# A first narrow cross-attention on one core: transposing the probabilities, or computing the scores twice

## The chip, the cores and the metric

The kernel is one program on one core of a Trainium2 chip. The metric is the device time of one execution, in microseconds (us); lower is better. TensorE (PE) multiplies matrices out of SBUF into PSUM, which has eight banks of 128 x 512 numbers; VectorE (DVE) and ScalarE (ACT) read PSUM; GpSimd (POOL) works on SBUF alone. The engines run side by side, each through its own instructions in order, and wait for each other by semaphores.

## The reference, cut to what matters

Four cross-attention layers follow each other on 32 batches of 128 tokens and 128 features, with a context of 128 x 96 per batch. The change is in the attention of the second layer, which has 16 heads of 8 features:

```python
q = (x @ Wq + bq)   # heads of 8: q[h], k[h], v[h]
k = (xf @ Wk + bk)
v = (xf @ Wv + bv)
scores = einsum('bhqd,bhkd->bhqk', q * SCALE, k)
probs = softmax(scores, axis=-1)
attn = einsum('bhqk,bhkd->bhqd', probs, v)
out = attn @ Wo + bo
```

Then come a layer norm, a feed-forward and the residual, which the change leaves alone. All numbers are float32.

## The kernel before

The program has four stages: the two wide attentions of the first layer (`wide_attention`), its feed-forward, the narrow attention of the second layer (`narrow_attention`, called with `L1` tiles) with its feed-forward, and the last two layers together (`wide_and_narrow`). The change replaces `narrow_attention`, which nothing else calls.

`narrow_attention` is a software pipeline over the batches. In step t each engine does its part of several batches, and each engine's list of parts is written out by hand in a function `step`; a loop (`pipeline`, `Fori`) runs two steps per turn between a written-out beginning and end. The steps' parts are these:

- POOL copies x of batch t+3 (`copy_rows`, L1231) and its context (`stage_context`, L1236), and makes `k_apart` of batch t+2 (`set_keys_apart`, L1242): four copies of the keys, in copy j all rows zero but those of head j of each group of four heads.
- PE transposes x (`transpose_h`, L1077), projects queries, keys (L1048, L1049) and values (L1054), and makes the scores of batch t+1 (`score`, L1028): four matmuls of 32 rows by 512 columns, one in each 32-row group of the array, into four banks.
- DVE takes the row maxima of 16 heads in two halves (`row_maxima`, L1167), negates the first half (L1174) and subtracts the second half from the scores (`subtract_maxima`, L1178).
- ACT takes the exponentials, the first eight heads one at a time with the maximum as bias (L1120), the other eight in one instruction (L1127). The result has queries on the partitions.
- PE transposes the 16 probability tiles (`transpose_probs`, L1040), and ACT copies them out, four tiles per copy (`turned_probs`, L1113).
- PE multiplies by a tile of ones for the sums and by the values (`weigh`, L1069: 16 matmuls each, four column groups of the array at a time). DVE inverts the sums (L1191) and multiplies (L1194). PE applies Wo (L1081), and DVE adds the bias into `y` (L1203).

Four PSUM banks hold the scores; the other four are a ring (`Ring`), filled in the order of the list `order`. PE may fill a ring bank once the engine that reads its earlier content has emptied it.

Of the kernel before, what the change touches and what calls it, by code (L numbers as in the profile page):

```python
# [19 lines left out]
HEADS = 16  # L20
# [113 lines left out]
def build(nc, a, out):  # L134
    ctx = ExitStack()
    with ctx:
# [797 lines left out]
def narrow_attention(nc, N, x, dst, ctxT, ident, head_mask, waits):  # L934
# [3 lines left out]
    order = [("T0", 0, "act"), ("T1", 0, "act"), ("Wo", -1, "dve"), ("T2", 0, "act"), ("T3", 0, "act"),  # L938
             ("qk", 2, "act"), ("v", 1, "dve"), ("hT", 3, "dve"), ("sum", 0, "dve"), ("PV", 0, "dve")]
    first, last = -3, BATCHES  # L940
    steady_first, steady_last = 3, BATCHES - 4
    ring = Ring(order, range(first, last + 1), BATCHES, {})
    GROUP = 4
    QUAD = DIM // 4
    SKEW = QUAD + NARROW

    def here(at, lag):
        return 0 <= at.n + lag < BATCHES

    with ExitStack() as ctx:  # L950
# [6 lines left out]
        rows_h = sb("rows_h", [TOKENS, DIM])  # L957
        hT = sb("hT", [DIM, 2, TOKENS])
        cT = sb("cT", [N.kv_rows, 2, TOKENS])
        qT = sb("qT", [128, 2, TOKENS])  # L960
        kT = sb("kT", [128, 2, TOKENS])
        k_apart = sb("k_apart", [128, 2, GROUP, TOKENS])
        v = sb("v", [TOKENS, 2, 4, 4 * SKEW])
        ones = sb("ones", [TOKENS, 4 * SKEW])
        invT = sb("invT", [128, TOKENS])
        oT = sb("oT", [128, TOKENS])
        probs = sb("probs", [TOKENS, 2, 2, SLOT_HEADS, TOKENS])
        probsT = sb("probsT", [TOKENS, HEADS, TOKENS])
        table_loader = sb("table_loader", [TOKENS, 1])
        row_max = sb("row_max", [TOKENS, 2, SLOT_HEADS])  # L970
        neg_max = sb("neg_max", [TOKENS, SLOT_HEADS])
        scores = ctx.enter_context(nc.psum_tensor(f"{N.name}_scores", [TOKENS, 2, 2, GROUP, TOKENS], FP32))
        ring_banks = ctx.enter_context(nc.psum_tensor(f"{N.name}_ring", [128, Ring.BANKS, BANK], FP32))

        filled = {"act": sem("ring_filled_act"), "dve": sem("ring_filled_dve")}
        emptied = {"act": sem("ring_emptied_act"), "dve": sem("ring_emptied_dve")}
        rows_h_ready = sem("rows_h_ready")
        cT_ready = sem("cT_ready")
        scores_full = sem("scores_full")
        max_ready = [sem("max_ready_0"), sem("max_ready_1")]  # L980
        neg_max_ready = sem("neg_max_ready")
        shifted = sem("shifted")
        exp_ready = [sem("exp_ready_0"), sem("exp_ready_1")]
        keys_apart = sem("keys_apart")
        cleared = sem("cleared")
        ones_ready = sem("ones_ready")
        block = ctx.enter_context(nc.Block())

        def bank(name, at):
            return ring_banks[:, ring.bank(name, at), :]  # L990

        def await_filled(engine, name, at):
            engine.wait_ge(filled[ring.engine[name]], ring.count(name, at))

        def await_emptied(engine, name, at):
            engine.wait_ge(emptied[ring.engine[name]], ring.count(name, at))

        def steps(engine, step):
            pipeline(engine, step, first, last, steady_first, steady_last)

        def by_group(tile):
            return tile.rearrange("p (j k) -> p j k", k=SKEW)

        @block.tensor
        def _(pe):
            keep_clock(nc, scores[:, 0, 0, 0, :], ident, START_COUNT)
# [3 lines left out]
            def start_fill(name, at):  # L1010
                before = ring.before(name, at)
                if before:
                    pe.wait_ge(emptied[before[0]], before[1])
                return bank(name, at)

            def filled_by(instruction, name):
                instruction.then_inc(filled[ring.engine[name]], 1)

            def score(at):
                pe.wait_ge(keys_apart, at.times(1, 1))  # L1020
                if at.n >= 1:
                    pe.wait_ge(exp_ready[0], at.times(2, 0))
                    pe.wait_ge(shifted, at.times(1, 0))
                p = at.n % 2
                for g in range(4):
                    r, s = divmod(g, 2)
                    part = slice(QUAD * g, QUAD * (g + 1))
                    last = nc.tensor.matmul(scores[:, s, r, :, :], qT[part, p, :], k_apart[part, p, :, :],  # L1028
                                            start=True, stop=True, tile_position=(QUAD * g, 0))
# [1428 lines left out]
```

## Time and profile before

| what | us |
|---|---|
| median of 3 runs (lowest, highest) | 1704.61 (1701.34, 1705.19) |
| profiled execution, span from first to last instruction | 1703.5 |
| the narrow attention of the second layer in it: first instruction 845.4, last row of y | 1060.0 |

No other time is given for the profiled execution, so its span stands for it: it is 1.1 us under the median and within the runs. The page of the profile gives busy times over the whole span; what belongs to the changed stage is read from views of the stretch from 845 to 1061 us. In rows of groups, "x32" counts instructions, then come busy us and mean ns, and behind the second bar the idle time in front of them. PE's records are matmuls; every float32 matmul has two records, since it runs as two passes, each with a weight load (PEld) of its own; a transpose has one.

### The profile page before, as it was taken

How to read it: one execution, taken by the hardware profiler on the slowest of the kernel's cores; microseconds unless marked ns; L12 is line 12 of the kernel's file. 1: busy time of each engine (PE TensorE's matmuls, PEld its weight loads, DVE VectorE, ACT ScalarE, POOL GpSimd, SP SyncE). 2: the span in 40 equal slices, each digit the busy share in tenths (PEclk: the TensorE clock that was granted, in tenths of full speed). 3: DMA queues.
4: the chain of work that ended last, by engine and by line, in shares of the span. 5: the costliest groups of instructions: out<-in, count | busy, mean ns of one | idle time of the engine just before them, and what ended most of it. 6: DMA issues, size and time to landing. Idle time of an engine off the chain costs nothing. (4 is left out here: it accounts for less than half of the span.)

```text
span 1703.5 us, 49104 instructions
## 1 busy us (share of the span) xinstructions
PE 1641.7 (96%) x16560; PEld 1355.9 (80%) x16560; DVE 1306.9 (77%) x2406; ACT 1244.3 (73%) x3865; POOL 677.1 (40%) x946
## 2 busy tenths in 40 slices
PE   7999999999999999989999998997999999999997
PEld 6888888888888888879877776876888888888876
DVE  5877777767777777747588887656888888888884
ACT  4777777767777777733388887446888888888886
POOL 3444444444444444423222221644444344443440
PEclk9999999999999999999989999999999999999999
DMA  6777777777776777630000000004443444344440
GB/s 183 199 195 188 188 188 186 210 201 210 197 186 186 186 183 196 186 95 1 0 2 0 0 0 1 1 13 140 125 141 116 142 126 139 118 140 122 133 130 8
DMA packets 225223, 211.27 MB, mean 124 GB/s; under 512 B 19474, under 2 KB 222804, under 8 KB 225108
## 3 DMA queue, kind: packets, MB, share of 16 engines
q1 hardware_dynamic: 225108, 209.92, 44.5%
q8 instruction: 49, 0.80, 0.2%
q14 instruction: 66, 0.54, 0.1%
HBM read 109.72 MB, written 100.14 MB: 123 GB/s over the span
## 5 line engine op out<-in xcount | busy, mean ns | idle before, releaser
L691 ACT ACTIVATE L_probs<-L_scores,L_neg_max 128x128 f32<-128x128 f32 x512 | 182.7, 386 | 135.7 <-DVE L_neg_max L783 135.7
L907 POOL TENSOR_TENSOR L_probs<-L_probs,L_inv_sum 128x1024 f32<-128x1024 f32 x128 | 242.8, 1897 | 88.7 <-DVE L_inv_sum L803 88.7
L777 DVE TENSOR_REDUCE L_row_max<-L_scores 128x8 f32<-128x1024 f32 x128 | 156.2, 1220 | 44.2 <-PE L_scores L549 44.2
L2122 POOL TENSOR_TENSOR L2L_w_probs<-L2L_w_probs,L2L_w_inv_sum 128x1024 f32<-128x1024 f32 x64 | 121.4, 1896 | 125.7 <-DVE L2L_w_inv_sum L1925 125.4
L809 DVE STREAM_TRANSPOSE L_squares<-L_probs 128x1024 f32<-128x1024 f32 x125 | 153.0, 1224 | 0.3 <-POOL L_probs L907 0.3
L549 PE MATMUL L_scores<-L_kT,L_qT 64*128 64x128 f32 x2048 | 132.5, 279 | 0.9 <-ACT L_kT L680 0.9
L600 PE MATMUL L_ring<-L_probsT,L_v 128*64 128x128 f32 x2048 | 127.5, 277 | 5.3 <-issue 2.5
L600 PEld LDWEIGHTS L_ring<-L_probsT,L_v 128*64 128x64 f32 x2048 | 111.2, 137 | 25.3 <-issue 20.3
L549 PEld LDWEIGHTS L_scores<-L_kT,L_qT 64*128 64x128 f32 x2048 | 120.1, 189 | 12.6 <-ACT L_oT L680 8.1
L793 DVE TENSOR_REDUCE L_sums<-L_probs 128x8 f32<-128x1024 f32 x64 | 78.1, 1220 | 66.3 <-ACT L_probs L698 66.3
L1689 ACT ACTIVATE L2L_w_probs<-L2L_scores,L2L_w_neg_max 128x128 f32<-128x128 f32 x256 | 90.4, 371 | 40.3 <-DVE L2L_w_neg_max L1889 40.3
L691 ACT ACTIVATION_READ_ACCUMULATOR L_probs<-L_scores,L_neg_max 128x1 f32 x512 | 115.8, 226 | 0.0
L680 ACT ACTIVATE L_oT<-L_ring 128x512 f32<-128x512 f32 x128 | 76.5, 599 | 42.0 <-PE L_ring L600 42.0
L1878 DVE TENSOR_REDUCE L2L_w_row_max<-L2L_scores 128x8 f32<-128x1024 f32 x64 | 76.6, 1197 | 24.4 <-PE L2L_scores L1444 24.4
L1700 ACT ACTIVATE L2L_n_probs<-L2L_scores,L2L_n_neg_max 128x128 f32<-128x128 f32 x256 | 90.7, 377 | 5.5 <-DVE L2L_n_neg_max L1895 4.9
L1242 POOL TENSOR_TENSOR L_k_apart<-L_kT,quad_mask 128x512 f32<-128x512 f32 x32 | 33.3, 1040 | 151.6 <-ACT L_kT L1113 151.6
L1113 ACT ACTIVATE L_probsT<-L_ring 128x512 f32<-128x512 f32 x128 | 75.3, 616 | 24.2 <-PE L_ring L1040 22.2
L1167 DVE TENSOR_REDUCE L_row_max<-L_scores 128x8 f32<-128x1024 f32 x64 | 78.1, 1220 | 18.9 <-PE L_scores L1028 18.9
L680 ACT ACTIVATE L_kT<-L_ring 128x512 f32<-128x512 f32 x128 | 76.8, 600 | 18.5 <-PE L_ring L557 18.5
L680 ACT ACTIVATE L_qT<-L_ring 128x512 f32<-128x512 f32 x128 | 76.2, 595 | 16.7 <-PE L_ring L557 11.4
L1040 PEld LDWEIGHTS L_ring<-ident,L_probs 128*128 128x128 f32 x512 | 57.0, 143 | 37.2 <-issue 21.3
L2098 POOL TENSOR_TENSOR L2L_n_x_bias<-L2L_n_rows_h,bias_L 128x128 f32<-128x128 f32 x32 | 14.6, 456 | 177.0 <-DVE x L1974 176.8
(227 smaller groups left out, 4644.1 us busy)
## 6 DMA issues: line engine op xcount, KB each, us to landing
L_relay<-L_squares SPq DMA_DIRECT2D x125, 512.0 KB, 3.4
L_probsT<-L_relay SPq DMA_DIRECT2D x500, 128.0 KB, 3.7
L2L_relay<-L2L_w_squares SPq DMA_DIRECT2D x62, 512.0 KB, 3.6
L2L_w_probsT<-L2L_relay SPq DMA_DIRECT2D x248, 128.0 KB, 2.9
out_x<-x SPq DMA_DIRECT2D x32, 64.0 KB, 2.7
L0a_wq<-in_L_xattn_Wq SPq DMA_DIRECT2D x2, 256.0 KB, 2.9
L0a_wk<-in_L_xattn_Wk SPq DMA_DIRECT2D x2, 256.0 KB, 3.7
L0a_wv<-in_L_xattn_Wv SPq DMA_DIRECT2D x1, 512.0 KB, 6.3
```

Source lines behind the costliest of these rows:

```text
L549: last = nc.tensor.matmul(scores[:, s, r, i, :], q[part, i, at.n % 2, :], k[part, i, at.n % 2, :], start=True, stop=True, tile_position=(h ...
L600: last = nc.tensor.matmul(to[WIDE * r:WIDE * (r + 1), TOKENS * i:TOKENS * (i + 1)], v[:, at.n % 2, WIDE * h:WIDE * (h + 1)], probsT[:, at. ...
L680: nc.scalar.activation(to, src, ACT.Copy).then_inc(emptied["act"], 1)
L691: done = nc.scalar.activation(slot_probs(at, 0)[:, n, :], scores[:, 0, r, i, :], ACT.Exp, scale=layer_of(at).scale, bias=neg_max[:, n:n + ...
L777: nc.vector.tensor_reduce(row_max[:, s, :], slot(s), AX.X, ALU.max).then_inc(max_ready[s], 1)
L793: nc.vector.tensor_reduce(sums[:, :, 1, :], slot_probs(at, 1).rearrange("p (r i) k -> p r i k", r=2), AX.X, ALU.add).then_inc(sum_ready, 1)
L809: nc.vector.transpose(squares[:, at.n % 2, :, SLOT_HEADS * s:SLOT_HEADS * (s + 1), :] .rearrange("p j h a -> p h j a"), slot_probs(at, s). ...
L907: nc.gpsimd.tensor_tensor(to, to, inv_sum[:, :, s, :].unsqueeze(3) .to_broadcast([TOKENS, 2, GROUP, TOKENS]), ALU.mult).then_inc(divided, 1)
L1167: nc.vector.tensor_reduce(row_max[:, s, :], scores[:, s, :, :, :].rearrange("p r i k -> p (r i) k"), AX.X, ALU.max).then_inc(max_ready[s], 1)
L1689: done = nc.scalar.activation(w_slot(at, 0)[:, h, :], scores[:, 0, r, i, :], ACT.Exp, scale=W.scale, bias=w_neg_max[:, h:h + 1], accum_out ...
L1700: done = nc.scalar.activation(n_slot(at, 0)[:, h, :], scores[:, 0, r, i, :], ACT.Exp, scale=N.scale, bias=n_neg_max[:, h:h + 1], accum_out ...
L2122: nc.gpsimd.tensor_tensor(to, to, w_inv_sum[:, :, s, :].unsqueeze(3) .to_broadcast([TOKENS, 2, GROUP, TOKENS]), ALU.mult).then_inc(w_divid ...
```

## The change

`narrow_attention` goes, and the second layer calls `text_attention`. It has the same inputs and outputs and does the softmax in another way:

- Scores are made a first time with queries on the partitions, only for the maxima (`scores_for_max`); DVE takes the maxima of four heads at a time, negated (`find_maxima`, 128 x 512).
- The 16 maxima per query are transposed (`turn_maxima`) and added into rows of the queries that were zero (`append_maxima`); the matching rows of `k_apart` are ones. A second matmul (`scores_less_max`) then gives the scores less their maximum directly, with keys on the partitions: what ACT's exponential makes of them (`exponentiate`, four heads each) goes into the product with the values without a transpose.
- The values have a column of ones, so one product (`weigh`) gives sums too. Its result is transposed back (`turn_back_and_out`), divided on rows (`divide_and_finish`), transposed again (`turn`) and multiplied by Wo.
- Three PSUM banks take scores for the maxima, three scores less maxima, one (`a_bank`) in turn the product, the transposes and the projections for ACT, and one (`b_bank`) the maxima and the transposes back for DVE.
- PE's step begins with two mixed passes (`both_scores`) right behind each other: the first makes groups 0 and 1 of the first scores of batch t+2 and groups 2 and 3 of the second scores of batch t, the second the other groups.
- The 40 steps are written out; there is no loop.

The core of the diff:

```diff
-            narrow_attention(nc, text, x, y, ctxT, ident, quad_mask, [(loaded["L1"], loads["L1"])])
+            text_attention(nc, text, x, y, ctxT, ident, quad_mask, [(loaded["L1"], loads["L1"])])
...
-def narrow_attention(nc, N, x, dst, ctxT, ident, head_mask, waits):
...
+def text_attention(nc, N, x, dst, ctxT, ident, quad_mask, waits):
...
+    S_BANKS = T_BANKS = 3
+    T_ORDER = (2, 3, 0, 1)
+    STEPS = range(-5, BATCHES + 3)
...
+            def scores_for_max(b, g, h):
+                part = slice(QUAD * g, QUAD * (g + 1))
+                if h == 0:
+                    if g == 0:
+                        pe.wait_ge(parts_ready, b + 1)
+                    if 4 * b + g >= S_BANKS:
+                        pe.wait_ge(max_ready, 4 * b + g + 1 - S_BANKS)
+                last = nc.tensor.matmul(s_bank(b, g)[:, 2 * (1 - h):2 * (1 - h) + 2, :],
+                                        q_part[part, b % 4, h, :], k_apart[part, b % 4, 2 * h:2 * h + 2, :],
+                                        start=True, stop=True, tile_position=(QUAD * g, 0))
+                if h == 1:
+                    last.then_inc(s_full, 1)
+
+            def scores_less_max(b, g, j):
+                part = slice(QUAD * g, QUAD * (g + 1))
+                if j == 0:
+                    pe.wait_ge(b_empty, nth_b["mT", b - 1])
+                    if t_nth(b, g) >= T_BANKS:
+                        pe.wait_ge(exp_ready, t_nth(b, g) + 1 - T_BANKS)
+                last = nc.tensor.matmul(t_bank(b, g)[:, j, :], k_apart[part, b % 4, j, :],
+                                        q_part[part, b % 4, j // 2, :],
+                                        start=True, stop=True, tile_position=(QUAD * g, 0))
...
+            def both_scores(t, s_groups, t_groups):
+                for h in range(2):
+                    if real(t + 2):
+                        for g in s_groups:
+                            scores_for_max(t + 2, g, h)
+                    if real(t):
+                        for j in (2 * h, 2 * h + 1):
+                            for g in t_groups:
+                                scores_less_max(t, g, j)
...
+            def weigh(t):
+                b = t - 1
+                pe.wait_ge(exp_ready, 4 * b + 4)
+                pe.wait_ge(a_empty, nth_a["PV", t] - 1)
+                for half in range(2):
+                    for e in range(2):
+                        for c in range(4):
...
+            def turn(t):
+                if nth_a["turn", t] > 1:
+                    pe.wait_ge(a_empty, nth_a["turn", t] - 1)
+                if real(t + 5):
+                    last = nc.tensor.transpose(a_bank[:, 0, :], x[:, t + 5, :], ident[:, :])
+                if real(t - 2):
+                    pe.wait_ge(b_empty, nth_b["D", t - 1])
+                    last = nc.tensor.transpose(a_bank[:, 1, :], rows_o[:, :, :].rearrange("p h d -> p (h d)"),
+                                               ident[:, :])
+                last.then_inc(a_full, 1)
...
+            def project(t):
+                pe.wait_ge(a_empty, nth_a["qkv", t] - 1)
...
+            for t in STEPS:
+                both_scores(t, (0, 1), (2, 3))
+                both_scores(t, (2, 3), (0, 1))
+                if ("mT", t) in nth_b:
+                    turn_maxima(t)
+                if ("PV", t) in nth_a:
+                    weigh(t)
+                if ("turn", t) in nth_a:
+                    turn(t)
+                if ("D", t) in nth_b:
+                    turn_back_and_out(t)
+                if ("qkv", t) in nth_a:
+                    project(t)
...
+            def exponentiate(b, g):
+                act.wait_ge(t_full, t_nth(b, g) + 1)
+                nc.scalar.activation(exps[:, b % 2, GROUP * g:GROUP * (g + 1), :].rearrange("p h q -> p (h q)"),
+                                     t_bank(b, g).rearrange("p j q -> p (j q)"), ACT.Exp,
+                                     scale=N.scale).then_inc(exp_ready, 1)
...
+            for t in STEPS:
+                if real(t):
+                    exponentiate(t, 2)
+                    exponentiate(t, 3)
+                    exponentiate(t, 0)
+                if ("PV", t) in nth_a:
+                    weighed_out(t)
+                if real(t):
+                    exponentiate(t, 1)
+                if ("turn", t) in nth_a:
+                    turned(t)
+                if ("qkv", t) in nth_a:
+                    projected(t)
...
+            for t in STEPS:
+                if real(t + 2):
+                    find_maxima(t + 2, 0)
+                    find_maxima(t + 2, 1)
+                if ("mT", t) in nth_b:
+                    append_maxima(t)
+                if real(t + 2):
+                    find_maxima(t + 2, 2)
+                if ("D", t) in nth_b:
+                    divide_and_finish(t)
+                if real(t + 2):
+                    find_maxima(t + 2, 3)
...
+            def set_parts(b):
+                pool.wait_ge(a_empty, nth_a["qkv", b - 4])
+                if b >= 4:
+                    pool.wait_ge(t_full, 4 * (b - 4) + 4)
+                for j in range(GROUP):
+                    other = (j + 2) % GROUP
+                    nc.gpsimd.tensor_scalar(k_apart[:, b % 4, j, :], qk[:, b % 2, 1, :], quad_mask[:, j:j + 1],
+                                            quad_mask[:, other:other + 1], ALU.mult, ALU.add)
+                for n in range(2):
+                    done = nc.gpsimd.tensor_scalar(q_part[:, b % 4, n, :], qk[:, b % 2, 0, :], half_mask[:, n:n + 1],
+                                                   half_bias[:, n:n + 1], ALU.mult, ALU.add)
+                done.then_inc(parts_ready, 1)
```

`weighed_out`, `turned` and `projected` are ACT's copies out of `a_bank`: 128 x 256, 128 x 256, and 128 x 128 with 128 x 256. Each of the product, `turn` and `project` waits until ACT has copied the one before it out (`a_empty`).

## Rows read from the trace of the kernel before

**Rows 1.** Tile y; busy time in a stretch: us, busy us and count by engine, granted clock

```profile
L1203 DVE TENSOR_TENSOR y<-L_ring,bias_L x32: 283/292/293, 866.9 to 1060.0; 128x128 f32 x26, 128x128 f32<-128x128 f32 x6
...
852.00:1061.00 209.00, 201.12 (x3097) 154.53 (x3094) 178.85 (x288) 179.22 (x479) 46.04 (x90) 0.98 0.00 1
```

**Rows 2.** Timeline of the beginning of the stage (start us, us, then the group)

```profile
847.27 0.14 PEld L1077 LDWEIGHTS L_ring<-ident,L_rows_h 128*128 128x128 f32 x1
847.38 0.27 PE L1077 MATMUL L_ring<-ident,L_rows_h 128*128 128x128 f32 x1
...
850.49 2.09 PE L1028 MATMUL L_scores<-L_k_apart,L_qT 32*128 32x512 f32 x8 [1.63 <-POOL L_k_apart L1242]
```

**Rows 3.** Timeline of one step

```profile
952.95 1.14 PE L1028 MATMUL L_scores<-L_k_apart,L_qT 32*128 32x512 f32 x8
...
954.74 1.04 PE L1040 MATMUL L_ring<-ident,L_probs 128*128 128x128 f32 x8
...
957.55 1.06 PE L1069 MATMUL L_ring<-L_probsT,L_v 128*32 128x128 f32 x32
```

**Rows 4.** Groups of instructions by line and shape, 852 to 1061 us

```profile
L1167 DVE TENSOR_REDUCE L_row_max<-L_scores 128x8 f32<-128x1024 f32 x64 | 78.1, 1220 | 18.9 <-PE L_scores L1028 18.9
L1113 ACT ACTIVATE L_probsT<-L_ring 128x512 f32<-128x512 f32 x128 | 75.3, 616 | 24.2 <-PE L_ring L1040 22.2
L1178 DVE TENSOR_TENSOR L_probs<-L_scores,L_row_max 128x1024 f32<-128x1024 f32 x32 | 39.2, 1225 | 1.1
L1191 DVE RECIPROCAL L_invT<-L_ring 128x128 f32<-128x128 f32 x32 | 30.4, 949 | 2.4 <-PE L_ring L1069 2.4
L1113 ACT ACTIVATE L_kT<-L_ring 128x128 f32<-128x128 f32 x31 | 8.8, 284 | 0.0
```

**Rows 5.** Waits from 852 to 1061 us: total us, times, longest

```profile
DVE L_row_max L1167 <- PE L_scores L1028: 18.9, 32, 3.5
```

**Rows 6.** One line's instructions: ns min/median/max, first and last start

```profile
L836 DVE COPY L_probsT<-L_ring x3: 692/692/692, 729.8 to 744.3; 128x512 f32<-128x512 f32 x3
```

**Rows 7.** Groups of the whole program, by line and shape

```profile
L2372 DVE SCALAR_TENSOR_TENSOR L0ff_hidden<-L0ff_value,bp,L0ff_gelu 128x256 f32<-128x256 f32 x64 | 29.6, 478 | 12.5 <-ACT L0ff_gelu L2322 9.5 <-PE L0ff_value L2283 2.3
L803 DVE RECIPROCAL L_inv_sum<-L_sums 128x8 f32<-128x8 f32 x128 | 23.4, 183 | 2.8 <-ACT L_probs L691 0.4
L698 ACT ACTIVATE L_probs<-L_probs 128x1024 f32<-128x1024 f32 x64 | 67.4, 1052 | 0.0
L1231 POOL COPY L_rows_h<-x 128x128 f32 x26 | 7.6, 294 | 0.0
L2414 POOL TENSOR_TENSOR L0ff_rstd<-L0ff_var_eps,minus_half 128x2 f32<-128x2 f32 x16 | 11.3, 704 | 1.3
```

**Rows 8.** The page's DMA queues: packets, MB, share of 16 engines

```profile
q8 instruction: 49, 0.80, 0.2%
```

**Rows 9.** Timeline at the end of the stage

```profile
1059.14 0.29 DVE L1194 TENSOR_TENSOR L_oT<-L_ring,L_invT 128x128 f32<-128x128 f32 x1
1059.48 0.30 PEld L1081 LDWEIGHTS L_ring<-L_wo,L_oT 128*128 128x128 f32 x2 [0.80 <-DVE L_oT L1194]
...
1060.01 0.29 DVE L1203 TENSOR_TENSOR y<-L_ring,bias_L 128x128 f32<-128x128 f32 x1 [0.58 <-PE L_ring L1081]
```

**Rows 10.** Timeline of the wide attention: column-tiled matmuls, then row-tiled ones

```profile
720.52 1.97 PE L600 MATMUL L_ring<-L_probsT,L_v 128*64 128x128 f32 x32
...
722.41 1.86 PEld L549 LDWEIGHTS L_scores<-L_kT,L_qT 64*128 64x128 f32 x32 [0.17 <-issue]
722.41 2.06 PE L549 MATMUL L_scores<-L_kT,L_qT 64*128 64x128 f32 x32
```

**Rows 11.** Busy time by stretch, columns as in the first group

```profile
850.40:854.40 4.00, 3.88 (x15) 1.97 (x15) 1.72 (x3) 0.63 (x3) 0.29 (x3) 0.50 0.01 4
1680.00:1690.00 10.00, 7.15 (x80) 5.44 (x79) 9.21 (x13) 8.65 (x35) 1.04 (x1) 1.00 0.01 1
```

More of the change, by code:

```diff
@@ L931, in _, with real, numbered @@
             steps(pool, step, before_loop)
-def narrow_attention(nc, N, x, dst, ctxT, ident, head_mask, waits):
[L938 to L942, printed above, removed]
+def text_attention(nc, N, x, dst, ctxT, ident, quad_mask, waits):
     GROUP = 4
     QUAD = DIM // 4
-    SKEW = QUAD + NARROW
-    def here(at, lag):
-        return 0 <= at.n + lag < BATCHES
+    SKEW = 48
+    SPAN = 2 * NARROW
+    PAIRS = HEADS // 2
+    S_BANKS = T_BANKS = 3
+    T_ORDER = (2, 3, 0, 1)
+    STEPS = range(-5, BATCHES + 3)
+    def real(b):
+        return 0 <= b < BATCHES
+    def numbered(parts):
+        return {name_t: n + 1 for n, name_t in enumerate(
+            (name, t) for t in STEPS for name, lags in parts if any(real(t + lag) for lag in lags))}
+    nth_a = numbered((("PV", (-1,)), ("turn", (5, -2)), ("qkv", (4, 1))))
+    nth_b = numbered((("mT", (1,)), ("D", (-1, -3))))
     with ExitStack() as ctx:
@@ L955, in sem @@
             return ctx.enter_context(nc.semaphore(f"{N.name}_{name}"))
[L957 to L966, printed above, removed]
@@ L1016, in filled_by @@
[L1016 to L1029, printed above, removed]
-                last.then_inc(scores_full, 1)
@@ L1106, in _ @@
-            steps(pe, step)
+            def scores_for_max(b, g, h):
[10 more added lines that the diff above has]
+                    last.then_inc(s_full, 1)
@@ new lines, in weigh @@
+            def weigh(t):
[5 more added lines that the diff above has]
+                        for c in range(4):
+                            pair = 4 * half + c
+                            last = nc.tensor.matmul(a_bank[QUAD * c:QUAD * (c + 1), half, :],
+                                                    v[:, b % 2, pair, :, :].rearrange("p e k -> p (e k)")
+                                                    [:, QUAD * e:QUAD * (e + 1)],
+                                                    exps[:, b % 2, 2 * pair + e, :],
+                                                    start=e == 0, stop=e == 1, tile_position=(0, QUAD * c))
+                last.then_inc(a_full, 1)
@@ new lines, in turn_back_and_out @@
+            def turn_back_and_out(t):
+                pe.wait_ge(b_empty, nth_b["D", t] - 1)
+                if real(t - 3):
+                    pe.wait_ge(a_empty, nth_a["turn", t - 1])
+                    last = nc.tensor.matmul(b_bank[:, 2, :], hoT[:, (t - 1) % 2, 1, :], N.wo[:, :],
+                                            start=True, stop=True)
+                if real(t - 1):
+                    pe.wait_ge(a_empty, nth_a["PV", t])
+                    for half in range(2):
+                        last = nc.tensor.transpose(b_bank[:, half, :], weighed[:, half, :], ident[:, :])
+                last.then_inc(b_full, 1)
@@ L1110, in _ @@
             nc.scalar.activation(table_loader[:, :], ident[:, 0:1], ACT.Exp)
-            def copied(to, src):
-                nc.scalar.activation(to, src, ACT.Copy).then_inc(emptied["act"], 1)
-            def exponentiate_0(at, r):
-                if r == 0:
-                    act.wait_ge(neg_max_ready, at.times(1, 1))
-                for i in range(GROUP):
-                    n = GROUP * r + i
-                    done = nc.scalar.activation(probs[:, at.n % 2, 0, n, :], scores[:, 0, r, i, :], ACT.Exp,
-                                                scale=N.scale, bias=neg_max[:, n:n + 1])
-                done.then_inc(exp_ready[0], 1)
@@ L1153, in _, with weighed_out @@
-            steps(act, step)
+            def exponentiate(b, g):
[3 more added lines that the diff above has]
+                                     scale=N.scale).then_inc(exp_ready, 1)
+            def weighed_out(t):
+                act.wait_ge(a_full, nth_a["PV", t])
+                nc.scalar.activation(weighed[:, :, :].rearrange("p b q -> p (b q)"),
+                                     a_bank[:, 0:2, :].rearrange("p b q -> p (b q)"), ACT.Copy).then_inc(a_empty, 1)
@@ L1260, in wide_and_narrow @@
+            for b in range(BATCHES):
+                set_parts(b)
 def wide_and_narrow(nc, W, N, x, ctxT, ident, minus_half, eps, head_mask, waits, store):
```

307 lines of the change are left out of this document (103 added, 204 removed).

## The prediction

> **What bounds the kernel now.** I found the stage by its output: y's 32 rows start from 866.9 to 1060.0 us [rows 1], so a step takes (1060.0 − 866.9)/31 = 6.23 us. Then the busy times of the stretch, in the same group: PE 201 of 209 us, DVE and ACT 179 each, POOL 46, no DMA. PE's figure is too high, since its records contain the way out of the array. One transpose takes 0.27 [rows 2], eight in a row 1.04 [rows 3]: a pass of 128 columns holds the array for (1.04 − 0.27)/7 = 0.11 us and needs 0.16 more to come out. In the same group the scores (eight passes of 512 columns, 1.14) are two rounds of 0.43, so four passes run together, one in each row group; the product with the values (32 passes, 1.06) is eight rounds of 0.11. PE's need per step is thus 16 × 0.11 for transposed probabilities, 0.86 for scores, 2 × 0.88 for sums and values and nine passes of 0.11 for the rest: 5.4 us. DVE has 179/209 × 6.23 = 5.3 us, of it two maxima at 1.22, the subtraction at 1.23 and the reciprocal at 0.95 [rows 4]. What DVE waits for is mainly the scores, 18.9 us in 32 waits, 0.6 per step [rows 5]. DVE is the bound, nearly closed by that wait.
>
> **The change, engine by engine.** *DVE*: four maxima of 512 columns cost 0.69 each, as a 512-column copy out of PSUM does [rows 6] (half of 1.22, 0.61, is the low end). The two additions of maxima, 128 columns each: such an instruction takes 0.48 for 256 columns [rows 7], less 128 × (1.22 − 0.69)/512 = 0.13 gives 0.35. In the same group a reciprocal of 8 takes 0.18; with 0.95 for 128, one of 16 takes 0.23. y 0.29 [rows 1], the multiplication on rows the same. Sum 4.25, down from 5.3. *ACT*: four exponentials of 512 at 0.61 (a copy of 512 takes 0.616 [rows 4], and an exponential of 1024 takes 1.05 [rows 7], so the function costs nothing extra); three copies of 256 columns at 0.40, a third of the way from 0.284 for 128 to 0.616 for 512 [rows 4]; a copy of 128. Sum 3.9. *PE*: 16 transposes and the ones go; scores are made twice, 1.72 if four groups always run together; maxima 0.11, product 0.88, two transposes 0.22, two back and Wo 0.44, projections 0.66. Sum 4.0, down from 5.4. *POOL*: six instructions of 128 columns, between a copy's 0.29 and the dearest small operation's 0.70 [rows 7]: 1.7 to 4.2 us, I take 0.4 each. They have more than a step from a projection to the scores that need it, so they cost nothing; over 6.8 us they would be the bound, and no row comes near. No DMA moves, and SP's queue is not passed. The 40 steps written out add code; the instruction queue was busy for 0.2% [rows 8], so I take nothing, and as upper bound one more gap of issue per step, 0.17 as in [rows 10].
>
> **What sets the step afterwards** is no engine but a chain PE–ACT–PE, because `a_bank` is used three times per step and PE waits for ACT between uses, and because the second mixed pass waits for what the first starts. Prices of the links: DVE ends at 1059.43, PE's load starts 1059.48, and DVE has the result of two passes at 1060.01 [rows 9]: 0.58 = 0.05 handoff + 0.11 load + 0.22 + 0.16 out + 0.04. The load in front of a matmul that had to wait is seen bare in 847.27 to 847.38 [rows 2]. A change of the array's division costs too: column-tiled records end at 722.49, so the last stream at 722.33, and the row-tiled load starts at 722.41 [rows 10]: 0.09 + 0.11 = 0.20. From the end of the second mixed pass (0):
>
> - change 0.20, maxima transposed 0.11; change 0.20, product 0.88: 1.39
> - out 0.20, ACT's copy 0.40: 1.99 (ACT's third exponential is done by 0.8; the fourth runs behind this copy and hides)
> - handoff and load 0.16, two transposes 0.22, out 0.20, copy 0.40: 2.97 (the transposes back and Wo, 0.44, lie beside this copy)
> - 0.16, six projection passes 0.66: 3.79; change 0.20: 3.99. ACT's last copies end at 4.6, before they matter
> - first mixed pass 0.86: 4.85
> - out 0.20, maxima of group 0 on DVE 0.69, handoff and load 0.16: 5.90. Here PE stands before group 3 of the first scores: it has three banks, and the fourth group needs the bank of group 0 of the same batch. Behind this wait on PE's queue stand the second scores of groups 0 and 1 (which wait for the first exponential, 0.20 + 0.61 + 0.16 = 0.97 against 1.05), hence ACT's last two exponentials and the whole list above. DVE reaches those maxima in time: its divide ends at about 3.7, the last maxima at 4.4
> - rest of the second pass 0.86: 6.76.
>
> So the step is **6.8 us** against 6.23, although every engine has less to do: PE idles 2.8 us of it. Thirty of 40 steps are full. Before them PE must turn x, project, let POOL set parts and make two batches of scores, one thing behind the other, mostly at half clock as the old beginning does (scores at 2.09 instead of 1.14 [rows 2, 3], granted clock 0.50 [rows 11]): turn until 848.0, turn and projection until 849.9, POOL until 852.4, scores of batch 0 with the wait until 857.1, turn and projection until 859.8, batch 1 until 863.4, two turns: first full step at 865. After the full steps: step 30 lacks scores for maxima and four projection passes (6.3), step 31 (2.7 of scores), then two products' chains (7.4) until y: 16.3. y's last row would start at 865 + 30 × 6.8 + 16.3 = 1085.3, and did at 1060.0: **+25 us**. The profiled span, 1703.5, is 1.1 under the median; on the median this gives 1704.6 + 25 = 1730.
>
> Unknown is the mixed pass itself: the trace has no matmuls of 256 and 128 columns side by side in different row groups. Not below 0.86, since each group has four rounds' worth of columns; at most about 1.9, if two passes of one matmul must both start before the next matmul (0.22 + 0.22 per matmul of 256, 0.11 + 0.11 of 128, partly overlapped). I take 0.86, as four equal passes do run together [rows 3], and keep the rest for the range. A second doubt is whether weights of 128 columns load in time for passes of only 128. In the wide attention 32 passes in two row groups take 2.06, so 16 in each group follow at 0.11, with a load of 128 columns for each [rows 10]: the load is hidden behind the same group's pass. The Trainium skill (TensorE: Matmul & The Clock Gate, Part 3) says that a weight load overlaps matmuls in flight only where the row group differs. By that rule each of the second scores' passes would cost 0.22, a mixed pass 1.7 and the step 8.4; the row speaks against it.
>
> **Rivals.** *Mixed passes run less than four abreast*, because starts keep program order and a short matmul stands behind a long one's second pass. Mild (pairs regroup, 1.08): step 7.0, 865 + 210 + 16 = 1091, 1736 us. Full (1.9, the first scores of group 0 done at 1.3): step 7.85, 1761 us. For it: nothing in the trace shows unequal ones overlapping; against: rounds of four equal ones start together. The same page of the Trainium skill, in the same part, has matmuls strictly first in, first out. Chance 0.24.
>
> *Weight loads not hidden* in the mixed pass: step 8.4, 865 + 252 + 16 = 1133, 1778 us. This is the rule named above; by [rows 10] I give it 0.04.
>
> *The clock falls.* With PE streaming 4.0 of 6.8 us the granted clock could drop to 1.2 GHz as in the beginning; streams and loads double, the step is about 11.2, 1860 us. Against: 1680 to 1690 us has PE records for 7.2 of 10 us, and clock 1.00 [rows 11]. Chance 0.05.
>
> *Faster, by hidden changeovers.* If PE loaded weights across the three changes of division (3 × 0.20) and ahead of the waits (3 × 0.11), the step would be 6.76 − 0.93 = 5.8, the start 862: 862 + 175 + 16 = 1053, 1698 us. It decides below a step of 5.97, where 865 + 30 × 5.97 + 16 is 1060. For it: in a row of transposes no load shows; against: [rows 9, 10] show each exposed. Chance 0.06. With most of these savings, a step near 6.0, there is no change: 0.05.
>
> That the change doesn't do what it says I leave out: the transposes and the subtraction are gone from the code.
>
> **How the numbers follow.** Forecast 0.56; its own range is a step of 6.5 to 7.1, 1721 to 1739. The first rival reaches to 1761; with a little over half of the changeovers hidden the step is 6.2 and the time 1712. Range 1712 to 1762, which leaves out the load rule, the clock, faster and no change, 0.20. Smaller than 0.2% (3.4 us), about what a measurement of this kernel tells from nothing, counts as no change. Faster 0.06, same 0.05, slower 0.89.
>
> **What the changed profile would show.** Right: y's rows 6.8 apart; in each step a PE wait of about 1 us on DVE's maximum between the mixed passes, and two on ACT's copies of `a_bank`; DVE and ACT busy for under 70% of the stage; clock 1.00. Wrong: rows of y under 6 apart, mixed passes far longer than 0.9, POOL named as releaser, or clock 0.50 in full steps.

## The result, and the profile after

| | before | after |
|---|---|---|
| median, us (executions) | 1702.97 (4) | 1736.80 (4) |
| lowest to highest | 1700.52 to 1705.19 | 1729.53 to 1744.12 |
| ratio of the times, 95% interval | | 1.0208 [1.0167, 1.0250] |
| span of the profiled execution | 1703.5 | 1742.4 |
| last row of y of the stage in it | 1060.0 | 1097.0 |

The change costs 34 us, 2.1%; the forecast was 1730. The profiled execution of after took 1744.12, the longest of its four. Its span grew by 38.9; y's last row stands 37.0 later, and what follows it took 1.9 more. But the stage also began earlier there. It starts from the last rows of x, which DVE wrote at 844.33 before and at 839.15 after:

```profile
844.33 0.42 DVE L2379 TENSOR_TENSOR x<-L0ff_out,L0ff_base 128x256 f32<-128x256 f32 x1 [2.21 <-PE L0ff_out L2292]
...
839.15 0.42 DVE L2361 TENSOR_TENSOR x<-L0ff_out,L0ff_base 128x256 f32<-128x256 f32 x1 [2.21 <-PE L0ff_out L2274]
```

From there to y's last row the stage takes 215.7 us before and 257.9 after: it grew by 42.2 in this execution, and the part ahead of it was 5.2 shorter. That part is the same code; in the traces of the old attention below it ends at 838.3 to 844.3, so such a difference comes from the execution. Times of the stage are therefore counted from these rows of x where two traces are compared.

Tile y, first over the whole stage, then from 905 to 1000 us alone, and in the same stretch before:

```profile
L1193 DVE TENSOR_TENSOR y<-L_b_bank,bias_L x32: 227/227/290, 897.8 to 1097.0; 128x128 f32<-128x128 f32 x32
...
L1193 DVE TENSOR_TENSOR y<-L_b_bank,bias_L x13: 227/227/229, 911.4 to 993.4; 128x128 f32<-128x128 f32 x13
...
L1203 DVE TENSOR_TENSOR y<-L_ring,bias_L x15: 292/292/292, 904.8 to 994.0; 128x128 f32 x15
```

In the middle the rows stand (993.4 − 911.4)/12 = 6.83 us apart, and stood (994.0 − 904.8)/14 = 6.37 apart before (the forecast's 6.23 is an average with the lighter first and last steps). The second thing to see is at both ends: the first row came 30.9 later than in [rows 1]. A part of that is the deeper pipeline, which writes the row of batch b in step b + 3 and not in step b + 1; another part is the granted clock. Columns of the next view: stretch, us, busy us (instructions) of PE, PEld, DVE, ACT and POOL, granted clock, DMA share, GB/s.

```profile
852.00:862.00 10.00, 8.48 (x35) 5.27 (x33) 4.11 (x8) 0.98 (x4) 2.59 (x6) 0.50 0.00 0
862.00:872.00 10.00, 9.29 (x81) 7.79 (x82) 3.21 (x7) 3.40 (x9) 4.06 (x10) 0.50 0.00 0
872.00:884.00 12.00, 11.50 (x105) 8.67 (x106) 4.82 (x10) 4.47 (x10) 3.72 (x9) 0.50 0.01 3
884.00:897.00 13.00, 11.79 (x143) 9.18 (x138) 4.85 (x11) 4.80 (x11) 2.59 (x6) 0.65 0.01 1
...
905.00:1000.00 95.00, 83.19 (x1300) 65.44 (x1298) 51.13 (x124) 48.85 (x112) 36.29 (x84) 1.00 0.01 2
...
1064.00:1097.30 33.30, 27.50 (x333) 21.37 (x333) 9.55 (x30) 12.28 (x29) 1.39 (x4) 0.70 0.01 1
```

From 852 to past 884 TensorE ran at 1.2 GHz (0.50), through three full steps, and again in part of the end; the middle ran at 2.4 GHz (1.00), with DVE busy for 54% and ACT for 51% of it, against 86% each in [rows 1]. PE's records, which contain the way out of the array, fill 88% of it. No engine is full, and the waits between engines show in the step. One step of it in the timeline (start us, us, then the group; in brackets the idle time before and its releaser):

```profile
953.05 0.48 PE L1014 MATMUL L_s_banks<-L_k_apart,L_q_part 32*128 32x256 f32 x2
...
953.37 0.38 PE L1014 MATMUL L_s_banks<-L_k_apart,L_q_part 32*128 32x256 f32 x2
...
953.58 0.38 PE L1014 MATMUL L_s_banks<-L_k_apart,L_q_part 32*128 32x256 f32 x2
...
954.21 1.29 DVE L1175 TENSOR_REDUCE L_maxima<-L_s_banks 128x4 f32<-128x512 f32 x2 [0.83 <-PE L_s_banks L1014]
954.33 1.09 ACT L1119 ACTIVATE L_exps<-L_t_banks 128x512 f32<-128x512 f32 x2 [0.62 <-PE L_t_banks L1026]
954.96 0.18 PEld L1014 LDWEIGHTS L_s_banks<-L_k_apart,L_q_part 32*128 32x128 f32 x1 [0.71 <-DVE L_maxima L1175]
...
956.24 0.33 PE L1047 MATMUL L_b_bank<-ident,L_maxima 128*128 128x128 f32 x1
...
956.50 1.08 PE L1058 MATMUL L_a_bank<-L_exps,L_v 128*32 128x128 f32 x32
...
957.65 0.38 ACT L1125 ACTIVATE L_weighed<-L_a_bank 128x256 f32<-128x256 f32 x1 [0.83 <-PE L_a_bank L1058]
...
958.08 0.14 PEld L1069 LDWEIGHTS L_a_bank<-ident,x 128*128 128x128 f32 x1 [0.77 <-ACT L_weighed L1125]
...
958.56 0.38 ACT L1131 ACTIVATE L_hoT<-L_a_bank 128x256 f32<-128x256 f32 x1
...
958.99 0.30 PEld L1091 LDWEIGHTS L_a_bank<-L_hoT,L_wq 128*128 128x128 f32 x2 [0.27 <-ACT L_hoT L1131]
...
959.86 0.48 PE L1014 MATMUL L_s_banks<-L_k_apart,L_q_part 32*128 32x256 f32 x2
```

From 953.05 to 959.86 is 6.81. PE's three waits are where the forecast put them: 0.71 for the first maximum between the mixed passes (the forecast said about 1), 0.77 for ACT's copy of the product, 0.27 for its copy of the turned rows. In the waits of the whole stage (total us, times, longest) DVE waits for scores as in [rows 5], for longer, and now PE waits for DVE's maximum and for ACT's copies as well:

```profile
DVE L_maxima L1175 <- PE L_s_banks L1014: 35.0, 32, 3.3
...
PEld L_s_banks L1014 <- DVE L_maxima L1175: 22.5, 31, 1.5
PEld L_a_bank L1069 <- ACT L_weighed L1125: 20.4, 26, 1.0
...
PEld L_a_bank L1091 <- ACT L_hoT L1131: 10.0, 30, 1.1
```

### The profile page after: what moved, and what is told of

Same layout as the page of the kernel before. It is cut to its first block and busy times, and to the rows that moved or that the text cites. A ratio compares the mean times of both kernels' runs of the same rounds, so it can differ in the third digit from the quotient of the medians.

```text
span 1742.4 us, 47955 instructions
## 1 busy us (share of the span) xinstructions
PE 1662.4 (95%) x16432; PEld 1372.4 (79%) x16432; DVE 1247.9 (72%) x2406; ACT 1177.9 (68%) x3648; POOL 712.2 (41%) x1045
## 5 line engine op out<-in xcount | busy, mean ns | idle before, releaser
L777 DVE TENSOR_REDUCE L_row_max<-L_scores 128x8 f32<-128x1024 f32 x128 | 156.1, 1219 | 41.6 <-PE L_scores L549 41.6
L1175 DVE TENSOR_REDUCE L_maxima<-L_s_banks 128x4 f32<-128x512 f32 x128 | 84.7, 684 | 42.7 <-PE L_s_banks L1014 42.6
L1231 POOL TENSOR_SCALAR L_k_apart<-L_qk,quad_mask 128x128 f32<-128x128 f32 x128 | 55.5, 448 | 142.0 <-ACT L_qk L1146 142.0
L1119 ACT ACTIVATE L_exps<-L_t_banks 128x512 f32<-128x512 f32 x128 | 72.7, 595 | 54.4 <-PE L_t_banks L1026 54.4
L1014 PE MATMUL L_s_banks<-L_k_apart,L_q_part 32*128 32x256 f32 x512 | 97.8, 448 | 10.6 <-ACT L_exps L1119 8.2
```

The lines of the kernel that those rows point to most:

```text
L777: nc.vector.tensor_reduce(row_max[:, s, :], slot(s), AX.X, ALU.max).then_inc(max_ready[s], 1)
L1014: last = nc.tensor.matmul(s_bank(b, g)[:, 2 * (1 - h):2 * (1 - h) + 2, :], q_part[part, b % 4, h, :], k_apart[part, b % 4, 2 * h:2 * h + 2 ...
```

## The experiments

All times below were taken beside executions of the kernel before (medians 1700.6 to 1703.1); behind a time stand its ratio to them and the 95% interval. "The changed kernel" is after; diffs are against it unless they say otherwise.

### The changed kernel again, and with the clock held

> The changed kernel again, nothing edited, as the base for the others. My theory: the step stays 6.82 us, and what differs between executions (1730 and 1743 us so far) is only how long PE runs at half clock in the first and last steps of this stage; so a profile near 1730 shows a first stretch of granted clock 0.50 that ends some 10 us or more before the 893.3 of the profile seen, with y's rows still 6.82 apart in the middle. Rival: the step itself differs between executions (6.4 against 6.8 would be 13 us over 30 steps); then rows of y in the middle stand closer in a faster execution. Time: 1728 to 1746, median near 1737.

Five executions took 1729.66 to 1743.23, median 1739.06, ratio 1.0213 [1.0190, 1.0236]. The profiled one is the fastest of them. Its tile y, and its busy times by stretch, columns as above:

```profile
L1193 DVE TENSOR_TENSOR y<-L_b_bank,bias_L x32: 227/228/291, 893.0 to 1086.9; 128x128 f32<-128x128 f32 x32
```

```profile
872.00:884.00 12.00, 11.02 (x147) 8.58 (x147) 5.34 (x12) 5.00 (x11) 4.75 (x11) 0.77 0.02 4
884.00:897.00 13.00, 11.09 (x176) 8.67 (x164) 6.94 (x16) 6.54 (x16) 5.19 (x12) 1.00 0.00 1
```

Its clock is back at 1.00 about 15 us earlier (0.77 and 1.00 where the slower execution had 0.50 and 0.65), and y ends 10.1 earlier (the stage takes 246.8 us for 257.9). Its rows in the middle stand 6.82 apart but for two gaps of 6.97 and 6.96, so the step is not what differs.

> The changed kernel with 2 to 4 unused passes of 128 columns in front of each of PE's waits in the beginning (five steps) and in the last five steps of the stage; nothing else moves. My theory, half clock in the beginning and the end is what the forecast mis-sized: the granted clock stays 1.00 from 845 on, the first three full steps take 6.8 instead of 7.9, 10.3 and 10.6 (8.4 us less), the beginning itself 2 to 4 less, the end 2 to 5 less; first row of y 885 to 889 instead of 898; time 10 to 16 below the profiled 1744, so 1727 (1722 to 1733), and executions agree within 4 us. Rival one, the first full steps are slow for another reason (instructions not yet fetched, POOL's parts late): the clock is 1.00 but these steps still take 8 to 10; time within 4 us of the changed kernel's. Rival two, extra passes don't hold the clock: 0.50 as before, and the time is 1 to 4 us longer.

```diff
+            def warm(t, count):
+                if t < 0:
+                    keep_clock(nc, t_banks[:, 2, 0, :], ident, count)
+                if t >= BATCHES - 2:
+                    keep_clock(nc, s_banks[:, 0, 0, :], ident, count)
...
+                warm(t, 2)
                 if ("turn", t) in nth_a:
                     turn(t)
...
+                warm(t, 2)
                 if ("qkv", t) in nth_a:
                     project(t)
```

(Four more stand ahead of the first scores and of the second pass in the beginning, two ahead of the transposes back in the end.) Measured: 1728.01 (1726.62 to 1730.01), 1.0147 [1.0124, 1.0169]. Tile y, and the busy times of the beginning:

```profile
L1207 DVE TENSOR_TENSOR y<-L_b_bank,bias_L x32: 227/228/292, 884.7 to 1081.7; 128x128 f32<-128x128 f32 x32
```

```profile
842.00:852.00 10.00, 9.46 (x75) 7.98 (x74) 2.15 (x4) 1.70 (x6) 5.21 (x12) 1.00 0.00 0
852.00:862.00 10.00, 9.40 (x97) 7.30 (x96) 5.17 (x11) 3.13 (x9) 5.23 (x12) 1.00 0.01 2
```

The clock stayed at 1.00 but for 3.4 us each at 863 and 1064; the first rows of y came at 884.7, 13.1 earlier than in after's profile, and 6.8 apart from the first on. The median is 11.1 below the repeated changed kernel's, and the spread fell from 13.6 to 3.4 us. So holding the clock is worth about 11 us of the change's 36 here, and the clock is what makes executions differ.

25 us are left with the clock held, and the longer step is under half of them. In the profiles the stage takes 243.0 us against 215.7 before, 27.3 more. Of these 8.4 lie between x's last rows and step 0 (19.5, before 11.1 to the first transpose of batch 0's probabilities at 855.39), 10.9 in steps 0 to 29 (858.20 to 1061.28, before 855.39 to 1047.60), and 8.0 behind them. So the beginning and the end of the new pipeline, which is two steps deeper, cost more than its steps do; how much of the 8.0 is the unused passes' I did not measure on this version.

### The passes apart

> The second mixed pass is moved behind the product with the values, and ACT's third and fourth exponential behind its copy of the turned rows; the work is the same. My theory, the chain PE-DVE-PE between the passes and PE-ACT-PE through a_bank: mT and the product (1.39 with changes of division) lie in the 1.05 of waiting for the first maximum, and the second pass lies in the wait for ACT's copy of the product. Step: first pass 0.86, to the product's end 2.25, second pass 3.31, turn 3.73, out and copy and handoff 0.76 to 4.49, projections 0.66 and a change 0.20 to 5.35. So rows of y 5.35 to 5.6 apart, no wait of PE for a maximum in the middle of a step, the time 30 x (6.82 - 5.4) = 43 below the changed kernel's, about 1694 (1686 to 1701). Rival one, the work of PE or the loads of weights set the step: 6.6 or more, 1730. Rival two, the wait only moves (DVE's maxima or ACT's exponentials become late at another place): 6.2 to 6.5, 1719 to 1728.

```diff
                 both_scores(t, (0, 1), (2, 3))
-                both_scores(t, (2, 3), (0, 1))
                 if ("mT", t) in nth_b:
                     turn_maxima(t)
                 if ("PV", t) in nth_a:
                     weigh(t)
+                both_scores(t, (2, 3), (0, 1))
```

(On ACT the order becomes exponentials 2 and 3, `weighed_out`, `turned`, exponentials 0 and 1.) Measured: **1681.46** (1679.38 to 1681.70), 0.9869 [0.9848, 0.9891]: 58 below the repeated changed kernel, and 1.3% below before. Tile y from 905 to 1000 us, and the timeline of one step:

```profile
L1193 DVE TENSOR_TENSOR y<-L_b_bank,bias_L x18: 227/227/229, 909.7 to 999.0; 128x128 f32<-128x128 f32 x18
```

```profile
953.48 0.33 PE L1047 MATMUL L_b_bank<-ident,L_maxima 128*128 128x128 f32 x1
...
953.74 1.08 PE L1058 MATMUL L_a_bank<-L_exps,L_v 128*32 128x128 f32 x32
...
954.75 0.48 PE L1014 MATMUL L_s_banks<-L_k_apart,L_q_part 32*128 32x256 f32 x2
...
955.85 0.33 PE L1069 MATMUL L_a_bank<-ident,x 128*128 128x128 f32 x1
...
956.76 0.30 PEld L1091 LDWEIGHTS L_a_bank<-L_hoT,L_wq 128*128 128x128 f32 x2 [0.27 <-ACT L_hoT L1131]
```

Rows of y stand (999.0 − 909.7)/17 = 5.25 apart, 1.57 less for the same instructions: two of the three waits are gone, and the 0.27 for the turned rows is the one that is left. My count said 5.35. Both rivals fall, and the time lies under the range I gave. Between the kept traces the stage takes 193.1 us instead of the 246.8 of the faster changed execution, 53.7 less: 30 x 1.57 = 47 by the step, 3 more in the first of these steps, whose clock was back at 867 us, 11 earlier, and 4 in the beginning and the end.

> Both edits of the two kernels before this one: the mixed passes apart and unused passes in the beginning and the end. My theory has them independent: 43 from the step and 8 to 14 from the clock, about 1685 (1677 to 1692), 1% below the kernel before the change. Rival: the clock is gained by the denser steps anyway (the unused passes add nothing to the apart version): within 3 us of the apart version alone.

Measured: 1677.27 (1675.85 to 1682.94), 0.9854 [0.9831, 0.9876]. The median is 4 below the apart version, which itself had come 13 below its expectation, but the two intervals overlap, and in the kept traces the stage takes 192.2 us for 193.1. So the unused passes add far less than the 8 to 14 I gave them, and the rival is not excluded. The traces show why: y's first row came 3.9 earlier, counted from x's last rows (877.8 against 883.4, of which 1.6 lie ahead of the stage), but the unused passes at the end stretched the last seven rows by 3, where the apart version's clock had been 1.00 anyway.

> The version with the mixed passes apart and unused passes in the beginning only: in the version with both, those at the end made the last seven rows of y take 3 us longer (the apart version's clock was at 1.00 there already), while those in the beginning brought the first row from 883.5 to 877.8. My theory, both effects add: 1681.5 - 5.7 = 1676, or 1677.3 - 2.9 = 1674, so 1675 (1671 to 1680), and the last row of y at 1028 to 1029. Rival, without passes at the end the clock falls there: last row at 1031 or later, 1678 or more.

Measured, with the passes in the steps before step 0 alone: **1673.51** (1668.44 to 1677.72), 0.9829 [0.9806, 0.9852], 1.7% below the kernel before and the lowest median here, though its interval overlaps those of the two versions above. Rows of y run from 877.0 to 1027.1, and the stage takes 189.1 us: the 3 at the end came back, and the rival falls.

### What each wait of the chain is worth

The next three were executed once each (1743.23, 1736.47 and 1721.89), and their times contain how long the clock stayed down; they are read by the rows of y from 905 to 1000 us, where it was 1.00.

> The changed kernel with ACT's copy of the product out of a_bank made twice (the first into a spare tile), 0.38 us more of ACT in each step, ACT being busy for half of the time. My theory, PE stands before the turn until that copy ends: rows of y 7.20 apart instead of 6.82 (7.15 to 7.25), the stage 30 x 0.38 = 11 longer, PE's wait for the weighed tile 0.77 + 0.38 = 1.15. Rival, the wait is covered by something else that ends nearly as late (DVE's maxima, the fourth exponential, POOL's parts): under 7.0, the stage 0 to 5 longer.

```diff
+                nc.scalar.activation(spare[:, t % 2, :],
+                                     a_bank[:, 0:2, :].rearrange("p b q -> p (b q)"), ACT.Copy)
                 nc.scalar.activation(weighed[:, :, :].rearrange("p b q -> p (b q)"),
```

Tile y, and the timeline around the copy:

```profile
L1196 DVE TENSOR_TENSOR y<-L_b_bank,bias_L x13: 227/227/229, 909.5 to 994.7; 128x128 f32<-128x128 f32 x13
```

```profile
957.38 0.38 ACT L1126 ACTIVATE L_spare<-L_a_bank 128x256 f32<-128x256 f32 x1 [0.83 <-PE L_a_bank L1059]
957.66 0.38 ACT L1128 ACTIVATE L_weighed<-L_a_bank 128x256 f32<-128x256 f32 x1
...
958.09 0.14 PEld L1070 LDWEIGHTS L_a_bank<-ident,x 128*128 128x128 f32 x1 [1.05 <-ACT L_weighed L1128]
```

85.2/12 = 7.10 per step, 0.28 more, and PE's wait 1.05 instead of 0.77, 0.28 more. That is under the 7.15 I gave as the least: my 0.38 was the wrong price of the copy, as of two copies back to back the second starts 0.28 after the first. What ACT's queue got longer came out whole at the end of the step, with ACT busy for half of it: this link is on the chain.

> The changed kernel with the maximum of group 0 taken over 64 of each head's 128 columns (the other half is left out), so DVE's first maximum takes about 0.4 instead of 0.69. Between the passes two things end within 0.05 us of each other in the changed kernel's trace: that maximum (954.90) and the first exponential (954.88 to 954.93). My theory: the exponential takes its place, the step falls by 0 to 0.07 only (6.75 to 6.82), and the profile names ACT instead of DVE as what PE waits for there. Rival, DVE's maximum alone holds the second pass: 0.3 less per step, rows of y 6.5 apart, 9 us.

```diff
-                nc.vector.tensor_reduce(maxima[:, b % 2, g, :, 0:1].rearrange("p j d -> p (j d)"), s_bank(b, g),
+                nc.vector.tensor_reduce(maxima[:, b % 2, g, :, 0:1].rearrange("p j d -> p (j d)"),
+                                        s_bank(b, g)[:, :, 0:64 if g == 0 else TOKENS],
```

Tile y, and the timeline between the passes:

```profile
L1193 DVE TENSOR_TENSOR y<-L_b_bank,bias_L x14: 227/227/229, 906.4 to 993.5; 128x128 f32<-128x128 f32 x14
```

```profile
955.15 1.02 DVE L1175 TENSOR_REDUCE L_maxima<-L_s_banks 128x4 f32<-128x256 f32 x2 [0.83 <-PE L_s_banks L1014]
955.27 1.09 ACT L1119 ACTIVATE L_exps<-L_t_banks 128x512 f32<-128x512 f32 x2 [0.62 <-PE L_t_banks L1026]
955.63 0.18 PEld L1014 LDWEIGHTS L_s_banks<-L_k_apart,L_q_part 32*128 32x128 f32 x1 [0.44 <-DVE L_maxima L1175]
...
957.07 0.33 PE L1047 MATMUL L_b_bank<-ident,L_maxima 128*128 128x128 f32 x1
```

87.1/13 = 6.70 per step, 0.12 less, where I had said at most 0.07. PE's wait for the maximum fell from 0.71 to 0.44, so more than half of that gain was lost behind it: the second pass, from this load to the transpose of the maxima, took 1.44 (955.63 to 957.07) instead of 1.28. The profile goes on naming DVE, whose wait comes first, not ACT as I had said.

> The kernel before this one, and the first exponential of a step (group 2) over two of its four heads (the other two heads' are left out from the third batch on). Both waits between the passes shrink, by about 0.3 for DVE and 0.2 for ACT. My theory: the step falls by the lesser, rows of y 6.55 to 6.65 apart, 5 to 8 us in all. Rival, neither sets the start of the second pass (PE's own order or a load of weights does): 6.75 to 6.82.

```diff
+                count = GROUP // 2 if g == 2 and b >= 2 else GROUP
-                nc.scalar.activation(exps[:, b % 2, GROUP * g:GROUP * (g + 1), :].rearrange("p h q -> p (h q)"),
-                                     t_bank(b, g).rearrange("p j q -> p (j q)"), ACT.Exp,
+                nc.scalar.activation(exps[:, b % 2, GROUP * g:GROUP * g + count, :].rearrange("p h q -> p (h q)"),
+                                     t_bank(b, g)[:, 0:count, :].rearrange("p j q -> p (j q)"), ACT.Exp,
```

Tile y, and PE's wait for the maximum from 905 to 1000 us (total, times, longest):

```profile
L1194 DVE TENSOR_TENSOR y<-L_b_bank,bias_L x14: 227/228/229, 911.2 to 996.7; 128x128 f32<-128x128 f32 x14
```

```profile
PEld L_s_banks L1014 <- DVE L_maxima L1176: 6.7, 15, 0.4
```

Rows of y stand 6.55 apart but for two gaps of 6.70, 0.26 below the changed kernel, and PE's wait for the maximum is 6.7/15 = 0.45. The second pass is back at 1.28 to 1.31, but for the two steps with the longer gaps, where it takes 1.44. Only with both shorter does the step fall by what the maximum lost. So maximum and exponential hold the second pass together; shortening the maximum alone is worth 0.12, and moving the pass is worth more than shortening both.

### The loop that went

> The kernel before the change, with the loop over the steps of this stage written out as the changed kernel has it; the work is the same. The forecast took the written-out steps at nothing, with 0.17 a step as upper bound. My theory: within 3 us of before (1700 to 1706), rows of y 6.23 apart on average as before. Rival, written-out code is dearer: 30 x 0.17 = 5 us or more, 1708.

```diff
-            pipeline(engine, step, first, last, steady_first, steady_last)
+            for t in range(first, last + 1):
+                step(At(t))
```

Measured: 1695.95 (10 executions, 1690.79 to 1701.28), 0.9974 [0.9957, 0.9991]: neither, it is faster, by 4.7 us. Rows of y stand 6.12 to 6.13 apart instead of 6.35 to 6.38.

> The kernel before the change with VectorE's steps of this stage written out and all other engines in the loop. With every engine written out a step took 6.12 instead of 6.36, and the difference lay in front of two short instructions of VectorE (0.09 and 0.16 a step). My theory, VectorE's own issue in the loop costs it, as VectorE is the bound: rows of y 6.12 to 6.16 apart. Rival, another engine in the loop is late with what VectorE waits for there: 6.30 to 6.38.

> The reverse: VectorE in the loop, all other engines written out. My theory: rows of y 6.33 to 6.38 apart, as before. Rival, the other engines' loop is what costs: 6.12 to 6.16.

One execution each took 1695.34 and 1699.84. The line of y from 905 to 1000 us with VectorE written out, then with all others written out (DVEq is VectorE's queue, not the engine):

```profile
L1207 DVE TENSOR_TENSOR y<-L_ring,bias_L x15: 283/284/284, 909.5 to 995.3; 128x128 f32<-128x128 f32 x15
```

```profile
L1207 DVEq FUSED_REGOPS  x15: 75/75/75, 905.6 to 995.2; - x15
L1207 DVE TENSOR_TENSOR y<-L_ring,bias_L x15: 292/292/292, 905.7 to 995.3; 128x128 f32 x15
```

85.8/14 = 6.13 against 89.6/14 = 6.40: it is VectorE's own loop. In it each addition into y, whose address depends on the turn of the loop, has a register operation of 75 ns in front; VectorE was the bound, so that showed in the step. In the loop about 0.15 a step stands in front of the addition that is not there without it (the 75 ns, and 0.07 of idle time), 0.10 in front of the negated maxima and 0.09 in front of the multiplication (L1194); 0.12 of this comes back as a shorter wait for the scores (0.41 a step, 0.53 written out). What the other two pieces are is open.

## Why the prediction was right, and what it missed

**The bound and the sign: right.** DVE and ACT are busy for about half of the step (POOL has more to do, and hides it), and the step is longer. The passes apart show the cause: the same work in another order is 1.57 us shorter per step. But the step grew by 0.45, from 6.37, and not from the average of 6.23. That leaves the sum untouched, which counts y's last row.

**The step: right, 6.76 forecast and 6.82 measured.** Link by link, forecast against the step shown, each counted from load to load (of a change of 0.20 the last 0.11 are the load): first pass to the load behind the maximum 1.91, measured 1.91; from there to the maxima's transpose 1.06, 1.28; to the product 0.31, 0.26; the product until ACT has it 1.19, 1.15; the copy to the turn 0.45, 0.43; turn to its copy 0.53, 0.48; to the projections 0.45, 0.43; projections to the next pass 0.86, 0.87. One link is off by more than 0.05: the second mixed pass takes 0.22 more than the forecast's, as its groups start one behind the other (954.96, 955.06 and 955.25, where the first pass starts at 953.05 and 953.06); why is open. The other links give 0.17 of it back, so that the sum is this close is in part luck. (Of the second scores behind the wait, `scores_less_max` lets only group 1 wait for the first exponential, not groups 0 and 1; the sum does not use it.)

**The mixed pass: right at the low end for the first one.** Its unequal matmuls start 0.21 apart (953.37, 953.58) as equal ones would, and the maxima start 1.16 after its load, where the forecast with 0.86 for the pass has 0.11 + 0.86 + 0.20 = 1.17. The first rival falls. By the Trainium skill (TensorE: Matmul & The Clock Gate, Part 3) weight loads overlap matmuls in flight only where the row group differs, which would have made a pass 1.7 and the step 8.4; the trace disagrees: with 128 columns to load for each pass of 128, the four groups still kept the pace of 0.21.

**POOL and other engines: right in effect.** POOL's six operations took 0.448 each, 2.7 per step instead of 2.4, hidden. The DVE and ACT prices hold (maxima 0.684 for 0.69, exponentials 0.595 for 0.61, copies of 256 at 0.38 for 0.40).

**The clock in the beginning and the end: the term that failed.** The forecast had half clock ahead of the full steps and none in or behind them. It kept the fall of the clock for a rival of the whole stage, and named a clock of 0.50 in full steps as a sign of being wrong; that sign came, for the first of them. The first full step came at 861.85 where the forecast has 865, but this is luck: the stage had begun 5.2 earlier than in the trace it was counted from, and from x's last rows to that step it took 22.7 instead of 20.7. Then the clock did not come back with the first full step. Steps 0 to 3 took 7.93, 10.32, 10.64 and 7.76 instead of 6.82, 9.4 us more, and the end, from step 30's second scores (1074.35) to the last row of y, took 22.7 instead of 16.3 (6.4 more; the forecast's three terms add up to 16.4). With 2.0 more at the start, 0.6 more from steps of 6.82 instead of 6.8, and 1.5 less in the last full steps, which already lack parts, the stage took 16.9 more than forecast. Less the 5.2 ahead of it, that is the 11.7 by which y's last row missed 1085.3. With the clock held, from the first full step (858.20) to the last row takes 223.5; the forecast's 30 x 6.8 + 16.3 is 220.3, and the unused passes at the end cost 3 in the apart version. So steps and end were counted right, at the clock they were counted for.

**The written-out steps: a gain in place of nothing or a small loss**, but without an effect on the sum: the forecast compared a chain of PE and ACT with a measured step of before. It changes what the step's growth means: against the old work without the loop (6.13) the two-pass form as ordered here costs 0.69 per step, and apart it gains 0.88.

## What to carry to other kernels

When a change takes work from every engine, sum the chain through the banks that are used more than once per step, wait by wait; then look whether work that is ready can be put into each wait before judging the idea, as one moved call of PE (with ACT's order to match) was worth 58 us here. Count the beginning and the end of a deeper pipeline as carefully as its step: with the clock held they were 16 of 27 us. Compare two traces of a stage from the stage's own start. Price the beginning of a stage at the clock that its waits will leave, and the first full steps too, until a row shows the clock back. Before an engine that is the bound is blamed for its work, look for register operations of a loop on its queue.

## What the runs showed of the hardware that I had not expected

- The half clock outlasted the first full steps: granted 0.50 with PE records for 11.5 of 12 us (872 to 884), while 83 of 95 us (905 to 1000) stayed at 1.00. At half clock records are longer (the transpose of the maxima 0.48 at 859.22, 0.33 at 956.24), so busy shares at the two levels cannot be compared.
- The length of that stretch differs from execution to execution of one kernel: the clock was back at 893 in one, and at 878 in the other, with the same instructions.
- A copy of 256 columns out of PSUM takes ACT 0.38 alone and adds 0.28 behind another one.
- With VectorE in the loop a step took about 0.25 us more (6.37 and 6.40) than with its steps written out (6.13).
